# Row normalisations of a feed-forward block on ScalarE instead of VectorE

## What is computed

```python
def _layernorm(x, axis=-1, eps=1e-05):
    m = jnp.mean(x, axis=axis, keepdims=True)
    v = jnp.var(x, axis=axis, keepdims=True)
    return (x - m) / jnp.sqrt(v + eps)

x = _layernorm(x + attn(x, ...), axis=-1)
x = _layernorm(x + ffn(x, w_gate, w_up, w_down), axis=-1)
# ffn: h = silu(x @ wg.T) * (x @ wu.T); out = h @ wd.T, hidden size 768
```

## Time and profile before

| | |
|---|---|
| median of 3 runs | 957.9 us (956.74 to 958.4) |
| profiled execution, its own time | 956.97 us |
| span of its trace | 955.2 us |
| PE busy | 875.8 us (92%) |
| DVE busy | 763.9 us (80%) |
| POOL busy | 644.8 us (68%) |
| ACT busy | 531.9 us (56%) |
| second block | from 634 us to the end |

### The profile page before, as it was taken

One profiled execution on the slowest core, in us unless ns is written; L12 is line 12 of the kernel. 1 busy time (PEld: TensorE's weight loads), 2 busy tenths in 40 slices (PEclk: granted clock), 3 DMA queues, 4 the chain that ended last, 5 costly groups with the idle time before them and its releaser, 6 DMA issues. The chain is left out here.

```text
span 955.2 us, 21723 instructions
## 1 busy us (share of the span) xinstructions
PE 875.8 (92%) x8204; PEld 673.7 (71%) x8204; DVE 763.9 (80%) x1319; ACT 531.9 (56%) x1049; POOL 644.8 (68%) x679
## 2 busy tenths in 40 slices
PE   4999999997999999999999999927899999999994
PEld 3888788876888888888888888613465565565563
DVE  3877777785889889888988888847688989988864
ACT  2655534345888888887887666305444444444441
POOL 3455444437889889889889889944667667667642
PEclk9999999998999999999999999976999999999998
DMA  6799689987667656766668885246123233231011
GB/s 223 230 309 314 189 270 304 308 247 236 173 176 200 183 160 191 200 172 172 189 197 249 242 249 168 93 146 221 45 91 109 68 95 104 66 94 60 24 45 44
DMA packets 171009, 163.61 MB, mean 171 GB/s; under 512 B 4320, under 2 KB 152800, under 8 KB 170272
## 3 DMA queue, kind: packets, MB, share of 16 engines
q1 hardware_dynamic: 169104, 153.64, 52.8%
q10 hardware_dynamic: 1808, 8.68, 2.7%
HBM read 119.57 MB, written 42.73 MB: 170 GB/s over the span
## 5 line engine op out<-in xcount | busy, mean ns | idle before, releaser
L647 POOL TENSOR_TENSOR gz<-prod 128x512 f32<-128x512 f32 x180 | 229.6, 1276 | 55.3 <-DVE prod L557 54.5
L557 DVE TENSOR_TENSOR prod<-bank,wfx 128x1024 f32<-128x1024 f32 x180 | 219.7, 1221 | 38.8 <-ACT bank L414 31.4
L329 PE MATMUL bank<-gz,ei 128*128 128x256 f32 x720 | 188.1, 384 | 7.7 <-POOL gz L647 7.5
L261 PE MATMUL bank<-wps,xs 128*128 128x512 f32 x768 | 180.7, 395 | 15.1 <-DVE wps L515 12.7
L261 PEld LDWEIGHTS bank<-wps,xs 128*128 128x128 f32 x768 | 144.7, 190 | 46.2 <-DVE wps L515 12.7
L414 ACT COPY bank<-bank 128x512 f32<-128x512 f32 x180 | 102.8, 571 | 117.5 <-PE bank L275 112.6
L1029 POOL TENSOR_TENSOR hl<-hf,hh 128x512 f16<-128x512 f32 x96 | 111.7, 1171 | 83.8 <-ACT hh L883 83.8
L657 POOL TENSOR_TENSOR y<-y,gate 128x256 f32<-128x256 f32 x192 | 142.3, 741 | 11.8 <-DMA gate<-gates 6.7
L275 PE MATMUL bank<-yh,ef 128*128 128x256 f16 x720 | 138.1, 274 | 3.1 <-ACT bank L414 2.1
L329 PEld LDWEIGHTS bank<-gz,ei 128*128 128x128 f32 x720 | 123.5, 192 | 21.7 <-POOL gz L647 12.2
L665 POOL TENSOR_TENSOR xs<-prod,xs 128x256 fp32r<-128x256 f32 x88 | 64.8, 747 | 76.5 <-ACT xs L395 76.0
(11 more groups left out here) (79 smaller groups left out, 1946.0 us busy)
## 6 DMA issues: line engine op xcount, KB each, us to landing
toep<-filter_rows SPq DMA_DIRECT2D x44, 1024.0 KB, 6.9
gates<-toep SPq DMA_DIRECT2D x48, 512.0 KB, 4.6
gate<-gates SPq DMA_DIRECT2D x48, 512.0 KB, 4.0
prod<-in_XT SPq DMA_DIRECT2D x22, 512.0 KB, 6.5
attn_out<-y SPq DMA_DIRECT2D x16, 512.0 KB, 5.6
ya<-attn_out SPq DMA_DIRECT2D x16, 512.0 KB, 4.7
xr<-in_X SPq DMA_DIRECT2D x16, 512.0 KB, 5.5
out_x<-oo SPq DMA_DIRECT2D x16, 512.0 KB, 3.4
```

The costliest lines, as they stand in the source:

```text
L261: mm = pe.matmul(b_proj[n % PBK][:, :], xs[:, n % XSS, hx, k, :], wps[:, hw, k, p * 512:(p + 1) * 512], start=(k == 0 and q == 0), stop=(k ...
L329: mm = pe.matmul(dst, ei[:, h, e0 * P:(e0 + 1) * P], gz[:, n % 3, h, :], start=False, stop=(h == 1))
L557: nc.vector.tensor_tensor(prod[:, n % 2].rearrange("p r j (c b) -> p r j c b", b=NB), b_copy[n % 2][:, :].rearrange("p (r c b) -> p r c b" ...
L647: nc.gpsimd.tensor_tensor(gz[:, n % 3], prod[:, n % 2, 0], prod[:, n % 2, 1], ALU.add).then_inc(gz_ready, 1)
```

## The change

The eight normalisations of a step leave DVE. ACT makes them as an Identity activation with a scale and a bias for each row: x * rs + nb, with nb = -mean * rs. POOL's root prepares nb with two more operations of 128x4: nb = mean * (-1) behind rs + eps, and nb = nb * rs behind the power. The semaphore rstd now counts the last of the four. ACT's norm1 of k+2 stands in two halves behind high 2 and high 3, its norm2 of k-1 behind high 5; at the start, norm1 of k=0 stands ahead of the weight casts and that of k=1 behind them. New waits keep buffers safe: POOL's root waits for the earlier normalisation that read rs (x1n_ready, oo_ready), DVE's bn_aggr for an earlier rstd, ACT ahead of silu 3 for zz_ready.

```diff
         @block.scalar
+            def normalise(dst, src, slot, b, done):
+                nc.scalar.activation(dst[:, b, :], src[:, b, :], ACT.Identity, bias=nb[:, slot, b:b + 1],
+                                     scale=rs[:, slot, b:b + 1]).then_inc(done, 1)
+
+            def norm1(k, r2, r3, count, parts):
+                act.wait_ge(rstd, count)
+                for b in parts:
+                    normalise(x1n[:, r3], x1[:, r2], 0, b, x1n_ready)
+
+            def norm2(k, r2, free, count):
+                act.wait_ge(out_done[r2], free)
+                act.wait_ge(rstd, count)
+                for b in range(NB):
+                    normalise(oo[:, r2], zz, 1, b, oo_ready)
...
                 silu(k, 2)
+                if ahead(k, 2) and not first(k):
+                    act.wait_ge(zz_ready, k * 2 + 1)
                 for m in range(3, HM):
                     silu(k, m)
                     high(k, r2, m - 1)
+                    if m < HM - 1 and ahead(k, 2):
+                        norm1(k + 2, r2, (r3 + 2) % 3, count1(k), range(2 * m - 6, 2 * m - 4))
                 high(k, r2, HM - 1)
+                if not first(k):
+                    norm2(k - 1, 1 - r2, free, count2(k))
...
+            norm1(0, 0, 0, 1, range(NB))
             for q in range(3):
...
+            norm1(1, 1, 1, 2, range(NB))
             step(0, 0, 0)
             rounds(act.Fori, step)
+            norm2(NA - 1, 1, NA // 2 * 16, 2 * NA)
...
         @block.vector
                 dve.wait_ge(stats, count)
+                if not isinstance(count, int):
+                    dve.wait_ge(rstd, count - 2)
+                elif count >= 2:
+                    dve.wait_ge(rstd, count - 1 if count < 5 or count >= 2 * NA - 2 else count - 2)
...
-            def normalise(dst, src, slot, count, done):
-                dve.wait_ge(rstd, count)
-                for b in range(NB):
-                    nc.vector.tensor_scalar(dst[:, b, :], src[:, b, :], mv[:, slot, b, 0:1], rs[:, slot, b:b + 1],
-                                            ALU.subtract, ALU.mult).then_inc(done, 1)
...
         @block.gpsimd
                 nc.gpsimd.tensor_tensor(rs[:, slot], mv[:, slot, :, 1], epst[:], ALU.add).then_inc(var_ready, 1)
+                nc.gpsimd.tensor_tensor(nb[:, slot], mv[:, slot, :, 0], minus[:], ALU.mult).then_inc(neg_ready, 1)
                 pool.wait_ge(var_ready, count)
-                nc.gpsimd.tensor_tensor(rs[:, slot], rs[:, slot], mhalf[:], ALU.pow).then_inc(rstd, 1)
+                nc.gpsimd.tensor_tensor(rs[:, slot], rs[:, slot], mhalf[:], ALU.pow).then_inc(root_ready, 1)
+                pool.wait_ge(root_ready, count)
+                pool.wait_ge(neg_ready, count)
+                nc.gpsimd.tensor_tensor(nb[:, slot], nb[:, slot], rs[:, slot], ALU.mult).then_inc(rstd, 1)
...
                 if ahead(k, 2):
+                    pool.wait_ge(x1n_ready, k * NB + 2 * NB)
                     root(0, count1(k))
...
                 if not first(k):
+                    pool.wait_ge(oo_ready, (k - 1) * NB + 1)
                     root(1, count2(k))
```

More of the change, by code:

```diff
@@ L706, in program @@
         rs = sb("rs", [P, 2, NB])
+        nb = sb("nb", [P, 2, NB])
+        minus = sb("minus", [P, NB])
         mhalf = sb("mhalf", [P, NB])
@@ L723, in program @@
         var_ready = sem("var_ready")
+        root_ready = sem("root_ready")
+        neg_ready = sem("neg_ready")
         rstd = sem("rstd")
@@ L883, in high @@
                 nc.scalar.activation(hh[:, r2, m, :], hf[:, m % 3, :], ACT.Copy).then_inc(hh_ready, 1)
+            def normalise(dst, src, slot, b, done):
[10 more added lines that the diff above has]
+                    normalise(oo[:, r2], zz, 1, b, oo_ready)
             def step(k, r2, r3):
+                free = 0 if first(k) else ((k - 1 - (1 - r2)) * 8 + 16)
                 silu(k, 0)
@@ L932, in stats1 @@
                 row_stats(x1[:, r2], 0, count)
-            def norm1(k, r2, r3, count):
-                normalise(x1n[:, r3], x1[:, r2], 0, count, x1n_ready)
             def split_x(k, r2):
@@ L965, in stats2 @@
                 row_stats(zz, 1, count)
-            def norm2(k, r2, free, count):
-                dve.wait_ge(out_done[r2], free)
-                normalise(oo[:, r2], zz, 1, count, oo_ready)
             def step(k, r2, r3):
-                free = 0 if first(k) else ((k - 1 - (1 - r2)) * 8 + 16)
                 product(k, 0)
@@ L982, in step @@
                 product(k, 2)
[L983 to L986, removed]
                 product(k, 3)
@@ L991, in step @@
                 product(k, 5)
-                if not first(k):
-                    norm2(k - 1, 1 - r2, free, count2(k))
+            nc.vector.memset(minus[:], -1.0)
             nc.vector.memset(epst[:], EPS)
@@ L1003, in _ @@
                 stats1(k, k, k + 1)
-                norm1(k, k, k, k + 1)
                 if k == 0:
@@ L1010, in _ @@
             stats2(NA - 1, 2 * NA)
-            norm2(NA - 1, 1, NA // 2 * 16, 2 * NA)
         @block.gpsimd
@@ L1035, in step @@
                 if ahead(k, 2):
+                    pool.wait_ge(x1n_ready, k * NB + 2 * NB)
                     root(0, count1(k))
                 if ahead(k, 3):
-                    pool.wait_ge(x1n_ready, k * NB + 2 * NB)
                     add(k + 3, 1 - r2)
@@ L1049, in _ @@
             root(0, 1)
+            pool.wait_ge(x1n_ready, NB)
             root(0, 2)
-            pool.wait_ge(x1n_ready, NB)
             add(2, 0)
@@ L1054, in _ @@
             rounds(pool.Fori, step)
+            pool.wait_ge(oo_ready, (NA - 1) * NB + 1)
             root(1, 2 * NA)
```

## The result

| | before | changed |
|---|---|---|
| median | 957.65 us (4 runs, 956.74 to 958.4) | 943.0 us (4 runs, 941.01 to 943.75) |
| profiled execution, its own time | 956.97 | 943.75 |
| span | 955.2 | 942.0 |
| first addition of the second block (L800, in the changed kernel L804) | 639.67 | 643.21 |
| from there to the end of the span | 315.53 | 298.79 |

The ratio is 0.9844, with a 95% interval of 0.9827 to 0.9862. The forecast was 941.3, the range 938.2 to 949.5.

A forecast was written before the change was run, and what follows sets the result against it. PE with a DVE detour of 1.33 us a step was taken to bound the second block; 956.97 -14.8 (steps) -3.4 (start) +0.5 (chain) +0.8 (k=14, 15) +1.0 (tail) = 941.1, said as 941.3 us, range 938.2 to 949.5.

The forecast's parts named there:

- steps to k=13, with the chain's excess: Second block's 13 down distances fall to PE's 16.47 us each, -14.8 us; ACT-POOL chain exceeding PE's work gives back 0.5.
- behind the last down: Tail after the last down: root +0.38 and four norms 2.05 on ACT against 1.38 on DVE, +1.0 us.
- What bounds the kernel: Second block's steps: PE with a 1.33 us DVE detour, from x1n slowed beside POOL's add; without it 16.47 us.
- ACT: Eight Identity operations a step on ACT, 0.49 us between starts, about 0.58 for one; +3.9 us a step, not full.
- POOL: POOL's root gets two 128x4 multiplications and grows from 1.27 to 1.65 us, +0.38; the first delays pow by 0.1.
- The new chain: Silu 3 over ACT and POOL to down: 8.36 us against PE's 8.45, just fitting; excess taken as 0.04 a step.
- The start: Start and step 0: ACT's early idle hides the move, x1n's 4.75 us go, new waits 2.2; -3.4 us.
- A: Late chain into down: small misjudgement of norm or root costs 0.3 to 0.6 a step, 945 to 949 us; 22%.
- B: ACT is the slower place: 0.8 us per normalisation, 10 us back, 951 us or more; 7%.
- C: POOL becomes the bound: root's small multiplications cost 1.01 each like pow and hold up down, 970 us; 4%.
- D: Table reloads on ACT if Identity is not in Silu's table: 6 loads of 1.28 a step, some 990 us; 1%.
- E: The stall was not x1n's and stays at hf, in step 0 too; some 959 us; 2%.

The follow-up runs named there:

- experiment 2: The changed kernel with norm1 back on DVE, so only norm2 on ACT and POOL's longer root kept; 965.37 us, ratio 1.0082 to the kernel before.
- experiment 3: The kernel before, nothing moved, POOL's add cut to one of the four rows of each partition; 939.0 us, ratio 0.9785.
- experiment 6: The kernel before, nothing moved between engines, POOL's add placed ahead of root instead of behind it; 947.05 us, ratio 0.9898.

## Why the prediction was right

Against the table's block lengths the terms of the sum can be read one by one. The measured values go by the first matmul of each down in the timeline, since the chain's start lies 0.17 behind it where PE doesn't wait:

| term | predicted | measured | from |
|---|---|---|---|
| steps to k=13, with the chain's excess | -14.8 +0.5 | -14.6 | 214.25 against 228.88 |
| start, to the first down | -3.4 | -3.6 | 35.60 against 39.24 behind the first addition |
| k=14 and 15 | +0.8 | +0.5 | 15.98 and 15.97 against 15.74 and 15.73 |
| behind the last down | +1.0 | +1.05 | 16.99 against 15.94 |
| second block | -15.9 | -16.7 | 298.79 against 315.53 |
| first block | 0 | +3.5 | 643.21 against 639.67 |

*What bounds the kernel.* Right: x1n's detour was the stall, and it was POOL beside it that made it, as experiments 2, 3 and 6 show from three sides. The prediction named only the add; low 2 behind it makes 0.8 of the 2.2 us.

*ACT.* The start distance of 0.49 came out as 0.50, 0.58 for one as 0.59. The operand price, +0.09 each from a 128x512 row, held for the bias too, which no row had shown.

*POOL.* Root was to grow by 0.38 and grew by 0.28. The two products take 0.20 each; they start 0.15 behind the operation before, and the first delays pow by 0.04 and not 0.1.

*The new chain.* Its place was right, and the 8.36 against 8.45 us came out as 8.35 against 8.44: root was 0.10 shorter than in the sum and the handover to PE 0.10 longer (0.23 instead of 0.13), which cancel. The margin is 0.09, so no excess was paid (+0.5 was too much). That the silus behind norm2 come late at no cost held too, even with four more operations on POOL: there PE's only data wait in the steps is down's for hl.

*The start.* ACT's timeline:

```profile
660.50 2.08 ACT L890 ACTIVATE x1n<-x,nb,rs 128x256 f32<-128x256 f32 x4 [3.65 <-POOL nb L1040]
662.59 1.28 ACT L883 ACT_TABLE_LOAD   x1
663.89 1.08 ACT L883 ACTIVATE sg<-bg 128x512 f32<-128x512 f32 x2
```

and PE's waits there:

```profile
664.54 0.39 PE L835 MATMUL bg<-xh,wq 128*128 128x512 f16 x1 [0.81 <-ACT sg L883]
...
670.12 0.39 PE L835 MATMUL bu<-xh,wq 128*128 128x512 f16 x1 [1.08 <-DVE hf L974]
...
678.81 0.28 PE L846 MATMUL bd<-wq,hh 128*128 128x256 f16 x1 [0.83 <-ACT hh L887]
```

The first silu comes 20.68 us behind the first addition; the forecast's 660.4 on the old scale is 20.73. The waits of step 0 are 1.08 and 0.83 and one of 0.15, 2.1 in all against 2.2, and no stretch at the low level follows them. The 0.81 ahead of 664.54 lies before them; that gate product starts 21.33 us behind the first addition, 21.66 before, and 21.3 to 21.5 was forecast. The granted clock of the ten microseconds from 663 and of the ten from 673 is 1.00, where before it was 0.86 from 660 and 0.83 from 670.

*The rivals.* A didn't come, by a tenth of a microsecond. B: ACT's operation is 0.50 from the next, not 0.8. The rule of the Trainium skill ("ScalarE: Activation LUTs", Rules for kernel authors), VectorE for such operations, holds for the operation alone (0.345 against 0.50) and not for this place, where DVE needed 0.9. C: the products are 0.20, not 1.01. But a longer root did make the loop slower where norm1 stayed on DVE, on another path than C's: it brought the add nearer to x1n (experiment 2). D: one table load. E: the stall is gone.

*Of luck* there is some. The sum gave 0.8 too little gain in the second block, and the first block's 3.5 us in the profiled run went the other way. The last down ran 7.08 us in both traces; one of 5.41 or 8.27, as other runs had, would have moved the number by 1.7 or 1.2 with the mechanism untouched. And the step from the sum's 941.1, for the profiled execution, to a median of 941.3 adds 0.2 where the 0.9 named beside it would give 942.0. The medians differ by 14.65 us.

## What to carry to other kernels

Where DVE's tensor_scalar on float32 in SBUF runs beside a POOL operation, read its duration at both places, alone and beside it, before asking which engine has too much work; the gain is in parting the two, by the order or by the engine. Moving the one stretched operation that PE waits for gave all of the gain, moving the other one none, and moving that alone a loss. When work goes to engines with idle time, add up the longest chain from the last shared point, with the handover as it is where the engine really waits: here it had 0.09 us to spare in a step of 16.5. Where the chain of waits names a round, look in the timeline whether an engine on it stood idle; if it did, the round had that much room. And before a few microseconds at an end are credited to an edit, compare the granted clock there.

## What the runs showed of the hardware

- Four tensor_scalar of 128x256 take 1.38 us alone, 2.22 to 2.27 beside one POOL operation of 1.16, 2.98 beside two, and 3.17 to 4.75 beside an add of 2.88 with an operation of 1.2 right behind it. POOL's add takes 2.85 to 2.90 either way; a low part that starts 0.3 us before x1n ends takes 1.32 instead of 1.16 (768.24 in experiment 6). The Trainium skill ("SBUF — State Buffer", Who interferes with whom) says that a DVE operation in a two-port mode, which tensor_scalar can enter, and a GpSimd operation lock each other out: whoever issues first has the shared ports for the whole of its operation. The traces agree for the times: the held operation goes on 0.07 to 0.08 us behind the end of POOL's, and with the add 0.3 us nearer ahead of it x1n takes 0.29 longer. Which mode it ran in no row names.
- Products, xl, zz and bn_stats on DVE keep their durations beside POOL (products 0.66 to 0.69 each, bn_stats 0.40 to 0.42, in the steps of both kernels).
- Experiment 6 ran six distances at 16.47 and six at 17.28 in one execution, with the same code: a loop of this kind can hold two paces. What tips it from one to the other was not tested.
- The last 48 matmuls, behind a pause of PE of 3.4 to 3.8 us, took 5.41, 7.08 and 8.27 us in different runs, with a granted clock of 1.00, 0.76 and 0.64.
- Identity with a scale and a bias for each row costs 0.50 us from start to start on 128x256, against 0.305 with constants, and needs no table load beside Silu.
